# An attention and mixture-of-experts kernel: clears taken off GpSimd, gates split by GpSimd, and another hand-written order of the first six periods

## What is computed

```python
q = proj_split(layernorm(x), W_Q); k = proj_split(ctx, W_K); v = proj_split(ctx, W_V)
scores = einsum('bhqd,bhkd->bhqk', q, k) / sqrt(16)
attn = softmax(scores, axis=1)                       # over the heads
x = x + einsum('bsd,ed->bse', merge(attn @ v), W_O)
y = layernorm(x)
logits = y @ Wr + br                                 # 8 experts, the best two get a gate
h = relu(einsum('btd,edh->bteh', y, W1) + b1)        # hidden size 256
out = x + einsum('bte,bteh,ehd->btd', gates, h, W2) + gates @ b2
```

## Time and profile before

| | |
|---|---|
| median of 3 runs | 209.44 us (209.28 to 210.56) |
| the profiled execution, its device time | 210.65 us |
| its span on the profile | 208.8 us |
| PE busy | 193.4 us (93%) |
| DVE busy | 175.0 us (84%) |
| ACT busy | 131.1 us (63%) |
| POOL busy | 119.3 us (57%) |
| moved by the transfers | 18.74 MB |
| granted PE clock | full in all 40 slices |

### The profile page before, as it was taken

One profiled execution on the slowest core, in us unless ns is written; L12 is line 12 of the kernel. 1 busy time (PEld: TensorE's weight loads), 2 busy tenths in 40 slices (PEclk: granted clock), 3 DMA queues, 4 the chain that ended last, 5 costly groups with the idle time before them and its releaser, 6 DMA issues.

```text
span 208.8 us, 4724 instructions
## 1 busy us (share of the span) xinstructions
PE 193.4 (93%) x1600; PEld 171.0 (82%) x1600; DVE 175.0 (84%) x472; ACT 131.1 (63%) x317; POOL 119.3 (57%) x143
## 2 busy tenths in 40 slices
PE   6799789998898989898999899989999999999995
PEld 6438776777697969895999789987999799799994
DVE  2889798899799997999898989898989997746643
ACT  3256727894587667595687668577676686545551
POOL 3724995996799916825772478446764975210100
PEclk9999999999999999999999999999999999999999
DMA  5957979025314232423051232322000000000000
GB/s 168 281 195 199 280 201 252 7 100 152 100 65 139 76 103 102 104 77 102 3 159 42 93 87 100 104 95 83 3 0 28 2 0 0 28 3 0 27 3 27
DMA packets 20360, 18.74 MB, mean 90 GB/s; under 512 B 1776, under 2 KB 18800, under 8 KB 20336
## 3 DMA queue, kind: packets, MB, share of 16 engines
q1 hardware_dynamic: 19904, 18.04, 30.3%
q10 hardware_dynamic: 432, 0.39, 0.6%
HBM read 11.88 MB, written 6.55 MB: 88 GB/s over the span
## 4 chain that ended last, share of the span: by engine, by line
PE 61%; DVE 23%; issue 6%; POOL 5%; ACT 3%; DMA 1%; DVEq 0%; ACTq 0%; POOLq 0%
PE y_ps L449 19%; PE h_ps L434 14%; PE misc_ps L390 6%; PE score_ps L371 5%; DVE attn L940 4%; PE h_ps L379 4%; DVE shift_m L932 3%; PE score_ps L359 3%; DVE acc L1028 2%; DVE gate_parts L1005 2%; PE score_ps L434 2%; PE score_ps L348 2%; POOL quarter_sum L1211 2%; PE misc_ps L399 2%; POOL half_sum L1209 1%
## 5 line engine op out<-in xcount | busy, mean ns | idle before, releaser
L449 PE MATMUL y_ps<-w_sb,hT 128*128 128x128 f32 x508 | 68.0, 276 | 1.5 <-DVE acc L1028 1.4
L703 ACT ACTIVATE hT<-h_ps,b_sb 128x256 f32<-128x256 f32 x118 | 49.4, 471 | 29.5 <-PE h_ps L434 29.5
L449 PEld LDWEIGHTS y_ps<-w_sb,hT 128*128 128x128 f32 x508 | 63.0, 191 | 3.9 <-issue 2.6
L1209 POOL TENSOR_TENSOR half_sum<-e_sb 128x512 f32<-128x512 f32 x28 | 36.8, 1314 | 27.7 <-ACT e_sb L675 27.7
L940 DVE TENSOR_TENSOR attn<-e_sb,e_rcp 128x1024 f32<-128x1024 f32 x32 | 44.6, 1402 | 0.2 <-ACT e_rcp L686 0.2
L932 DVE TENSOR_REDUCE shift_m<-score_ps 128x128 fp32r<-128x1024 f32 x32 | 38.3, 1210 | 1.2 <-PE score_ps L359 1.0
L675 ACT ACTIVATE e_sb<-score_ps 128x1024 f32<-128x1024 f32 x32 | 32.8, 1024 | 10.0 <-PE score_ps L371 9.8
L434 PE MATMUL h_ps<-x1T_hi,w_lo 128*128 128x256 f32 x118 | 37.2, 318 | 0.3 <-ACT hT L703 0.2
L1028 DVE SCALAR_TENSOR_TENSOR acc<-y_ps,gates,acc 128x128 f32<-128x128 f32 x96 | 29.1, 343 | 7.4 <-PE y_ps L449 5.8
L434 PE MATMUL h_ps<-x1T_hi,w_hi 128*128 128x256 f32 x118 | 32.9, 282 | 0.0
L1211 POOL TENSOR_TENSOR quarter_sum<-half_sum 128x256 f32<-128x256 f32 x28 | 31.3, 1118 | 2.2
(11 more groups left out here) (121 smaller groups left out, 280.3 us busy)
## 6 DMA issues: line engine op xcount, KB each, us to landing
k_scratch<-k_parts SPq DMA_DIRECT2D x14, 256.0 KB, 2.6
k_stack<-k_scratch SPq DMA_DIRECT2D x14, 256.0 KB, 3.8
q_stack<-q_scratch SPq DMA_DIRECT2D x28, 128.0 KB, 2.7
q_scratch<-q_parts SPq DMA_DIRECT2D x7, 256.0 KB, 2.2
w_sb<-in_w SPq DMA_DIRECT2D x1, 1024.0 KB, 7.9
out_y<-y_out SPq DMA_DIRECT2D x7, 128.0 KB, 1.9
x_all<-in_x SPq DMA_DIRECT2D x1, 768.0 KB, 6.7
ctxT<-in_ctx_t SPq DMA_DIRECT2D x1, 640.0 KB, 6.4
```

The lines of the kernel that those rows point to most:

```text
L449: mm = nc.tensor.matmul(product(j, t), hT[:, j % 2, c, t * P:(t + 1) * P], w2_sb[:, e * HC + c, :], start=(c == 0), stop=(c == HC - 1))
L703: op = nc.scalar.activation(hT[:, j % 2, c, :], hidden(j)[:, c * S:(c + 1) * S], ACT.Relu, bias=b1_sb[:, e * HC + c:e * HC + c + 1])
L1209: nc.gpsimd.tensor_tensor(half_sum[:], e[:, 0:HQ // 2], e[:, HQ // 2:HQ], ALU.add).then_inc(sum_step, 1)
```

## The change

Four things, none of which changes what is computed:

1. v_pad's four clears go from POOL to DVE: three before x arrives, the fourth into the middle of the first batch's experts. One half of q_stack is cleared by ACT, by a copy of the identity times 0. POOL clears the other half first of all.
2. The two operations that fill gate_parts go from DVE to POOL as `split_gates`. In `period` it stands behind the first head_sum. DVE's `transpose_gates` keeps only the transpose, and moves from right behind `make_gates` to behind `ln2`. POOL's `block_gates` moves from ahead of `ln2_end` to behind it.
3. The lists in `beginning` of PE, ACT, DVE and POOL are in another order.
4. The order of SP's list is the same, row for row; only the moments at which its waits are met can change.

```diff
@@ PE, beginning (start) @@
+                transpose_xn(0, None, 0)
                 project_k(0, None, 0)
-                project_v(0, None, 0)
-                transpose_xn(0, None, 0)
+                project_q(0, xnT_taken, 1)
                 project_k(1, k_first_made, 1)
-                project_q(0, xnT_taken, 1)
                 project_k(2, None, 0)
...
@@ ACT, before beginning @@
+            nc.scalar.activation(q_stack[:, 1].rearrange("p j o s -> p (j o s)").rearrange("p (n c) -> p n c", c=P),
+                                 ident[:].unsqueeze(1).to_broadcast([P, PAIRS * 2 * S // P, P]), ACT.Copy,
+                                 scale=0.0).then_inc(q_zeroed[1], 1)
@@ DVE @@
+            def zero_v(b):
+                nc.vector.memset(v_pad[:, b], 0.0).then_inc(v_zeroed, 1)
+
             def transpose_gates(b):
-                dve.wait_ge(gates_made, b + 1)
-                if b == 0:
-                    dve.wait_ge(gates_zeroed, 1)
-                nc.vector.tensor_copy(gate_parts[:].rearrange("p t (k s) -> p t k s", s=2 * E)[:, :, :, 0:E],
-                                      gates[:, b % 2].unsqueeze(2).to_broadcast([P, TT, 2, E])).then_inc(gate_step, 1)
-                dve.wait_ge(gate_step, 2 * b + 1)
-                nc.vector.tensor_tensor(gate_parts[:, :, E:2 * E], gates[:, b % 2], gate_parts[:, :, 0:E].bitcast(F32),
-                                        ALU.subtract).then_inc(gate_step, 1)
                 dve.wait_ge(gate_step, 2 * b + 2)
@@ DVE, period @@
                     make_gates(g)
-                    transpose_gates(g)
...
                     ln2(f)
+                if there(g):
+                    transpose_gates(g)
@@ DVE, beginning (start) @@
                 dve.wait_ge(x1_in, 16)
                 ln1(TT, 2 * TT, 1)
-                k_lo(1)
                 spread_q(0)
+                ln1_end(1, 1)
                 spread_q(1)
-                ln1_end(1, 1)
                 head_max(0, 0)
                 head_max(0, 1)
+                k_lo(1)
+                split_b2(0)
...
                 normalize(0, 1)
+                normalize(0, 2)
                 q_lo(2)
@@ DVE, before beginning @@
+            zero_v(0)
+            zero_v(1)
             dve.wait_ge(ident_made, 1)
...
+            zero_v(2)
             dve.wait_ge(x0_in, 32)
@@ POOL @@
+            def split_gates(b):
+                pool.wait_ge(gates_made, b + 1)
+                if b == 0:
+                    pool.wait_ge(gates_zeroed, 1)
+                wait(pool, gatesT_made, b)
+                nc.gpsimd.tensor_copy(gate_parts[:].rearrange("p t (k s) -> p t k s", s=2 * E)[:, :, :, 0:E],
+                                      gates[:, b % 2].unsqueeze(2).to_broadcast([P, TT, 2, E])).then_inc(gate_step, 1)
+                pool.wait_ge(gate_step, 2 * b + 1)
+                nc.gpsimd.tensor_tensor(gate_parts[:, :, E:2 * E], gates[:, b % 2], gate_parts[:, :, 0:E].bitcast(F32),
+                                        ALU.subtract).then_inc(gate_step, 1)
...
@@ POOL, period @@
                     head_sum(now, 0)
+                if there(g):
+                    split_gates(g)
+                if there(now):
                     head_sum(now, 1)
-                if there(g):
-                    block_gates(g)
                 if there(f):
                     ln2_end(f)
+                if there(g):
+                    block_gates(g)
@@ POOL, beginning (start) @@
-                zero_q(1)
-                zero_v(0)
-                ln1_rstd_of(TT, 2 * TT, 1)
                 zero_q(0)
+                iota8()
+                zero_gates()
+                ln1_rstd_of(0, TT, 0)
+                ln1_rstd_of(TT, 2 * TT, 1)
```

More of the change, by code:

```diff
@@ L533, in beginning @@
                 head_sum(0, 0, k_lo_made, 1)
-                transpose_xn(2, k_lo_made, 2)
                 subtract_max(0, 2)
                 head_sum(0, 1, log_made, 1)
-                project_q(2, xnT_taken, 3)
+                transpose_xn(2, k_lo_made, 2)
                 subtract_max(0, 3)
                 head_sum(0, 2, log_made, 2)
+                project_q(2, xnT_taken, 3)
+                head_sum(0, 3, log_made, 3)
+                project_v(0, None, 0)
                 scores(1, 0)
-                head_sum(0, 3, log_made, 3)
+                scores(1, 1)
@@ L542, in beginning @@
+                project_v(1, v_taken, 1)
+                attend_values(0, q_lo_made, 2)
                 subtract_max(1, 0)
-                project_v(1, v_taken, 1)
-                scores(1, 1)
+                project_out(0, heads_taken, 1)
+                subtract_max(1, 1)
                 scores(1, 2)
-                attend_values(0, q_lo_made, 2)
-                subtract_max(1, 1)
-                project_out(0, heads_taken, 1)
+                project_v(2, x1_made, 1)
+                scores(1, 3)
@@ L549, in beginning @@
+                transpose_x1n(0, v_taken, 3)
                 subtract_max(1, 2)
-                scores(1, 3)
-                project_v(2, x1_made, 1)
+                subtract_max(1, 3)
+                route(0, x1T_lo_made, 1)
+                expert_up(0, 0)
                 scores(2, 0)
-                subtract_max(1, 3)
-                transpose_x1n(0, v_taken, 3)
-                subtract_max(2, 0)
-                expert_up(0, 0)
-                route(0, x1T_lo_made, 1)
+                project_k(3, logits_made, 1)
@@ L566, in beginning @@
+                expert_up(0, 4)
                 scores(2, 2)
-                project_q(3, xnT_taken, 4)
-                expert_up(0, 3)
-                expert_down(0, 2)
                 scores(2, 3)
-                expert_up(0, 4)
                 expert_down(0, 3)
-                gated_b2(0, q_lo_made, 3)
                 expert_up(0, 5)
-                attend_values(1, b2_added, 1)
+                attend_values(1, q_lo_made, 3)
+                subtract_max(2, 2)
+                subtract_max(2, 3)
@@ L576, in beginning @@
+                gated_b2(0, heads_taken, 2)
+                expert_down(0, 4)
+                project_out(1, b2_added, 1)
                 expert_up(0, 6)
-                project_out(1, heads_taken, 2)
-                subtract_max(2, 2)
-                expert_down(0, 4)
-                subtract_max(2, 3)
+                scores(3, 0)
                 project_k(4, x1_made, 2)
-                scores(3, 0)
+                scores(3, 1)
                 expert_down(0, 5)
                 expert_up(0, 7)
+                transpose_x1n(1, k_lo_made, 4)
@@ L1232, in block_gates @@
                                         ALU.mult).then_inc(gates_blocked, 1)
-            def zero_v(b):
-                nc.gpsimd.memset(v_pad[:, b], 0.0).then_inc(v_zeroed, 1)
             def zero_q(slot):
@@ L1254, in period @@
                     head_sum(now, 0)
+                if there(g):
+                    split_gates(g)
+                if there(now):
                     head_sum(now, 1)
+                if there(f):
+                    ln2_end(f)
                 if there(g):
                     block_gates(g)
-                if there(f):
-                    ln2_end(f)
                 if there(now):
```

196 lines of the change are left out of this document (96 added, 100 removed).

## The result

The changed kernel takes 208.44 us (207.99 to 208.61, 8 runs) where the kernel before takes 209.27 us (8 runs beside it): ratio 0.9947, 95% interval 0.9929 to 0.9965. The forecast was 205.7. The sign was right and the time lies in the range, but the gain is 0.8 us, not 3.7: within 1%, so the case that was given 24%.

What follows compares the result with a forecast made beforehand. PE, busy 193.4 of 208.8 us with DVE close behind, bounds the kernel, so only its waits can be won. Terms -1.8 - 3.2 - 2.2 + 3.8 - 0.3 = -3.7 gave 205.7 us, range 201.6 to 209.8.

Steps and rivals of the forecast that it cites:

- the case that was given 24%: Whole kernel: the time stays within 1% of the kernel before; chance 0.24, beside 0.62 for faster and 0.14 for slower.
- The reference: Whole kernel: the profiled span 208.8 becomes 205.1, and the median 209.4, taken as 0.6 above the span, becomes 205.7 us.
- The start: Beginning: xn's pair falls from 2.33 to 0.59 us, first scores move from 9.78 to about 8.0: -1.8 us.
- The clears: Beginning: ACT's q_stack clear is hidden below about 2.4 us; three v_pad clears fall in DVE's idle time, the fourth counts 0.5.
- The second batch's scores: Batch 1: q lands at about 24.8; PE, doing head_sum and project_v(0) first, arrives at 24.0, waits 0.8, keeps 1.8 us.
- the second rival: Beginning: k spill issued 2.9 us later, q lands later than about 27, the middle's 3.2 go too: 211.8 us; 13%.
- The middle: Up to period 6: waits for expert add, b2 add and xnT go, LayerNorm 2 wait (1.2) comes: -3.2 us.
- The periods: From period 6 on: -2.2 for maxima, +3.8 for gated_b2, -0.3 for half of a 0.6 us wait.
- (a): Periods 6 to 8: gate_parts leaves DVE, so three 0.75 us PE waits for the second maximum go: -2.2 us.
- (b): Periods 6 to 10: block_gates behind ln2_end makes PE wait at gated_b2: +3.8 us, bounds +2.5 to +8.
- The first rival: The middle gives nothing: DVE is 84% busy and each removed wait returns on its list; 209.2 us; 20%.
- The sum: Whole kernel: -1.8 - 3.2 - 2.2 + 3.8 - 0.3 = -3.7 us.

Runs made afterwards that it cites:

- the first experiment: The kernel before, unchanged, profiled a second time: 209.31 us, span 207.5.
- experiment 11: The changed kernel with q_stack and v_pad cleared by GpSimd again, as before, all other orders kept: 211.55 us, ratio 1.0108.
- Experiments 9 and 10: 9: ACT's take_v(3) ahead of two inverses, on the second experiment's kernel, 204.03 us; 10: also PE's subtract_max(1, 2) ahead of transpose_x1n(0), 204.06 us.
- experiment 12: The ninth kernel with DVE's eight maxima of batches 2 and 3 reading four of eight heads: 202.67 us, ratio 0.9669.
- Experiments 2 to 4: 2: changed kernel, transpose_gates and block_gates early again, 203.66 us; 3: changed kernel, only block_gates early, 205.06; 4: kernel before with only the period edits from period 6, 210.68.
- the second experiment's kernel: The changed kernel with transpose_gates behind the add of expert 0 and block_gates ahead of ln2_end, split still on POOL: 203.66 us, ratio 0.9728.
- experiment 6: The changed kernel with the fourth head sum and project_v(0) put behind the first scores of batch 1: 209.87 us, ratio 1.0028.
- the ninth kernel: The second experiment's kernel with ACT's take_v(3) moved ahead of two inverses in the first six periods: 204.03 us, ratio 0.9746.

## Why the prediction was right and wrong

**The reference, about 1 us: wrong.** "The profiled span of 208.8 becomes 205.1, and the median of 209.4, which lies 0.6 above the span, 205.7." The span belonged to an execution of 210.65 us, 1.85 above it; the median belonged to executions whose span is about 207.5. The table ahead of the prediction had both numbers. A span of 205.1 means 206.95 us, not 205.7.

**The start, -1.8: half right.** The pair went from 2.33 to 0.60 us, as said, and the first scores came 1.43 us earlier than in the earlier trace rows (1.57 against the first experiment). What arrived at the second batch's scores is less. The changed kernel's PE there:

```profile
22.25 2.05 PE L379 MATMUL h_ps<-e_sb,ident 128*128 128x128 f32 x16
24.14 0.61 PE L337 MATMUL y_ps<-w_qkvo,ctxT 128*128 128x128 f32 x4
24.50 1.19 PE L359 MATMUL score_ps<-q_stack,k_stack 128*128 128x256 f32 x8
```

The fourth head sum stood behind these scores before and takes 24.14 - 22.25 = 1.89 us. The v projection did not: before, project_v(0) was the second step of PE's list and ran at 5.80, while xn was awaited. The prediction counted it with the head sum as moved from behind the scores; its 0.36 us are new ahead of them. So by the old count the scores stand at 24.50 - 1.89 = 22.61, against 23.59 in the usual execution of the kernel before: -1.0 us. With the clears back (experiment 11) the same point is 26.98 - 1.89 = 25.09, 1.5 later than in that execution: the new order alone costs 1.5 us there, since PE and ACT now have the late xn ahead of k and v(0) stands right ahead of these scores, and the clears bring 2.5. The step that failed is to carry the 1.74 us of the pair through unchanged. The Trainium skill, page "SBUF — State Buffer", section "SBUF: two separate sides", has a VectorE operation in a two-port mode and a GpSimd operation lock each other out for a whole instruction. The pair at 4.91 in experiment 11 agrees, 2.33 us against 0.60; the pair at 10.15 in the earlier trace rows, 0.59 us beside the other clear, does not, and why was not tested.

**The clears, 0: right.** ACT's clear took 1.89 us and ended at 5.06, before its first copy at 6.23; a v_pad clear on DVE takes 0.48 to 0.52.

**The second batch's scores: mechanism right, size wrong.** They came at 24.50 without a wait (forecast: at 24.0, waiting until 24.8). The landing at 24.8 was read from the earlier trace rows, the held-up execution; q lands at about 23.3. The reorder there is worth 1.4 us all the same. The k spill did go out 3.2 us later than the earlier trace rows has it, and landed 2.6 us after issue instead of 6.4:

```profile
12.30 1.25 SPq L210 DMA_DIRECT2D k_scratch<-k_parts  x2
...
DMA to landing us min/median/max: 2.5/2.6/2.6
```

So the second rival, which needed a q landing past 27, did not come. The first expert_down started at 38.80, as forecast (38.8), but that is luck: w2 landed 6.9 us after its issue at 30.71, at 37.6, and PE did not wait for it.

**The middle, -3.2: the term that failed most.** Counted with the 1.89 us above, the stretch from the second batch's scores to period 6 went from 80.38 - 23.59 = 56.8 to 77.82 - 22.61 = 55.2 us: -1.6, half of what was forecast. The three named waits did go (0.9, 1.1 and 1.2 us), the wait for x1n came as said (1.26), and so did three that were not foreseen: 0.8 for a maximum at 43.4, 0.5 at attend_values(1), 1.0 for v(3) at 64.6. PE's idle rows behind the second batch's first scores sum to 4.9 us in the first experiment, and all but 0.2 of them (at attend_values(0)) are gone in the changed kernel; but its own rows sum to 4.0, where the forecast named only the 1.2 for x1n and the fourth clear (0.5). That is 0.9 of the 1.6 us; the rest is mostly PE being shown busy 0.6 us less for the same work. The step that failed is to take a wait in this stretch as time that is won when its cause goes. Experiments 9 and 10 took away two more and won nothing. The first rival, "each wait taken away there comes back as another", was right by half, but not by the cause that it named: experiment 12 took 3.4 us off DVE's list and moved period 6 by 0.4.

**The periods, +1.3: right.** (a) the three waits for the maximum at 0.75 us became one of 0.5, where all were to go; (b) five waits of 0.41, 0.41, 0.8, 0.9 and 1.0 us, 3.6 in all for a forecast of 3.8. Experiments 2 to 4 confirm cause and size. Taking (b) back brings 4.8 us, a microsecond more than the waits themselves. The profiles place it. From period 6 on the second experiment's kernel takes 123.99 us, 4.4 less than the changed kernel (128.38): 3.6 us of waits, and 0.8 us that PE is busy less with the same 1064 matmuls (121.57 to 120.78), which fits the fill that is shown as busy behind a wait. The other 0.4 is the changed kernel's profiled execution, which lies that much under its median.

**The sum.** In spans: forecast -1.8 - 3.2 + 1.3 = -3.7; measured from 207.5 to 206.2, -1.0 - 1.6 + 1.3 = -1.3. Timed it is -0.8; the changed kernel's profiled execution was 0.4 us faster than its median.

## What to carry to other kernels

Before a sum is made against a profiled span, check how that execution stands to the median, and read no landing or wait off an execution that is a microsecond slower than the rest. Where an engine is busy 94% of a stretch and its waits are short and for different engines, a wait that is taken away tends to come back at the next hand-off (here 1.6 us arrived of 3.2 counted, and nothing of the two waits filled later). A wait that hangs on one late instruction in every period is different: moving that instruction gave its whole price back and more.

## What was not expected of the hardware

TensorE's granted clock fell behind one wait and not behind a nearly equal one at the same place. Windows of experiment 11 at the wait for x1n (1.43 us, until 35.75), then of the changed kernel at the same place (1.26 us, until 33.10); the granted clock is the third number from the right:

```profile
34.00:36.00 2.00, 0.57 (x6) 0.39 (x5) 1.97 (x2) 1.26 (x4) 1.84 (x4) 1.00 1.11 210
36.00:38.00 2.00, 1.91 (x11) 1.41 (x10) 0.45 (x2) 1.71 (x3) 1.92 (x3) 0.86 1.05 280
38.00:40.00 2.00, 2.00 (x10) 2.00 (x11) 1.69 (x10) 1.09 (x3) 1.84 (x4) 0.50 0.49 135
```
```profile
32.00:34.00 2.00, 0.90 (x5) 0.84 (x6) 1.35 (x3) 1.26 (x3) 1.92 (x3) 1.00 1.03 220
34.00:36.00 2.00, 1.91 (x14) 1.51 (x14) 1.06 (x7) 1.94 (x2) 1.84 (x4) 1.00 1.05 302
```

In experiment 11 the clock stood at 0.50, the lower of its two levels (1.2 GHz), at 38 to 40 us, and the first expert_down came 3.97 us later than in the changed kernel where the transpose before it came 2.65 us later. By period 6 it was 3.42 us. So the clock may have cost up to 0.8 us of that kernel's time (3.42 - 2.65); but one of its six runs had the full mean clock, and took 212.18 us against 211.43 to 211.62 of the five others. In experiment 6 one execution of twelve had the same mean clock as those five (0.992) and was the slowest, 210.77 us, beside one of 210.54 at the full clock. What decides it was not tested.

GpSimd's instructions stretch as DVE's do. In the ninth kernel the same addition of 256 elements takes 1.61 and 0.73 us within four microseconds, and the next one of 128 takes 0.46 and 1.32:

```profile
58.01 1.61 POOL L1213 TENSOR_TENSOR quarter_sum<-half_sum 128x256 f32<-128x256 f32 x1
59.69 0.46 POOL L1216 TENSOR_TENSOR e_sum<-quarter_sum 128x128 f32<-128x128 f32 x1
...
61.47 0.73 POOL L1213 TENSOR_TENSOR quarter_sum<-half_sum 128x256 f32<-128x256 f32 x1
62.28 1.32 POOL L1216 TENSOR_TENSOR e_sum<-quarter_sum 128x128 f32<-128x128 f32 x1
```

Each long one began beside a normalization on DVE (57.07 to 59.01 and 61.84 to 63.28). The split of the gates, whose second operation had been up to 1.28 us on DVE, took 0.21 and 0.22 us on GpSimd in six of the eight batches; in the other two its first operation took 1.20 and 1.14 us there.
